# Order of the score products: mask passes first, then row scores, then transposed scores

## The reference

```python
q = query @ wq + query @ Aq @ Bq * 4.0; k = query @ wk; v = query @ wv + query @ Av @ Bv * 4.0
q, k = apply_rope(q), apply_rope(k)                       # per head
scores = einsum('bhqd,bhkd->bhqk', q, k) / sqrt(16)
scores = where(key > query, -1e9, scores)                 # causal
x = layernorm(x + einsum('bhqk,bhkd->bhqd', softmax(scores), v) @ wo)
h = butterfly(gelu(butterfly(x @ W_exp + b_exp, up) + up_bias), down)
x = layernorm(x + h @ W_con + b_con + down_bias)
```

## Time and profile before

| | us |
|---|---|
| median of 3 runs | 1261.94 (1259.41 to 1267.34) |
| the profiled execution, whole | 1255.18 |
| its span on the core | 1253.4 |
| PE busy | 1126.7 (90%) |
| DVE busy | 835.4 (67%) |
| ACT busy | 677.8 (54%) |
| POOL busy | 472.8 (38%) |

### The profile page before, as it was taken

One profiled execution on the slowest core, in us unless ns is written; L12 is line 12 of the kernel. 1 busy time (PEld: TensorE's weight loads), 2 busy tenths in 40 slices (PEclk: granted clock), 3 DMA queues, 4 the chain that ended last, 5 costly groups with the idle time before them and its releaser, 6 DMA issues.

```text
span 1253.4 us, 27298 instructions
## 1 busy us (share of the span) xinstructions
PE 1126.7 (90%) x8462; PEld 787.5 (63%) x8462; DVE 835.4 (67%) x1955; ACT 677.8 (54%) x1067; POOL 472.8 (38%) x536
## 2 busy tenths in 40 slices
PE   4467789999999999999999999999999999989876
PEld 3344456766666666766666666767666666656565
DVE  5497867575767776676767767675767677665332
ACT  1256647465564747465664747365655747474601
POOL 2231334435353444444253434444353434332311
PEclk8678879999999999999999999999999999999989
DMA  5745453645556454644556454645555565641201
GB/s 201 176 143 141 120 146 96 187 122 156 122 148 174 137 154 112 188 124 157 114 165 148 141 151 118 195 112 170 122 165 123 145 164 138 162 117 37 76 21 34
DMA packets 94983, 169.90 MB, mean 136 GB/s; under 512 B 14872, under 2 KB 36120, under 8 KB 94944
## 3 DMA queue, kind: packets, MB, share of 16 engines
q1 hardware_dynamic: 93888, 166.53, 49.3%
q10 hardware_dynamic: 832, 1.83, 0.4%
q0 software_dynamic: 224, 1.04, 0.2%
HBM read 92.28 MB, written 77.07 MB: 135 GB/s over the span
## 4 chain that ended last, share of the span: by engine, by line
PE 73%; DVE 17%; issue 6%; DMA 2%; ACT 2%; POOL 1%; DVEq 0%; POOLq 0%; SPq 0%; ACTq 0%
PE ps_m L516 24%; PE ps_m L659 18%; PE ps_m L629 9%; PE ps_t L601 9%; PE ps_s L558 5%; PE ps_m L638 5%; DVE m_raw L851 4%; PE ps_s L587 2%; DVE m_raw L846 2%; DVE stats L907 2%; DVE x_res L922 1%; DVE rope_in L870 1%; DVE m_pad L860 1%; DVE x1T_lo L878 1%; DVE mv L912 1%
## 5 line engine op out<-in xcount | busy, mean ns | idle before, releaser
L732 ACT ACTIVATE pT<-ps_t 128x512 f32<-128x512 f32 x640 | 345.9, 599 | 275.8 <-PE ps_t L601 275.4
L851 DVE TENSOR_REDUCE m_raw<-ps_s 128x1 f32<-128x512 f32 (+2 forms) x768 | 345.1, 504 | 158.6 <-PE ps_s L587 157.8
L993 POOL TENSOR_SCALAR_AFFINE_SELECT pT<-pT 128x512 f32<-128x512 f32 (+1 forms) x320 | 174.9, 551 | 418.2 <-ACT pT L732 416.0
L659 PE MATMUL ps_m<-w,gact 128*128 128x256 f32 x1024 | 240.4, 386 | 1.8 <-ACT gact L800 1.1
L659 PEld LDWEIGHTS ps_m<-w,gact 128*128 128x128 f32 x1024 | 188.6, 190 | 31.2 <-ACT gact L800 1.5
L558 PE MATMUL ps_s<-k_st,q_st 48*128 48x512 f32 (+3 forms) x1024 | 136.5, 324 | 42.9 <-DVE m_raw L851 24.3
L601 PE MATMUL ps_t<-q_st,k_st 50*128 50x512 f32 (+3 forms) x1024 | 169.0, 388 | 0.5 <-ACT pT L732 0.4
L629 PE MATMUL ps_m<-pT,v_aug 128*32 128x512 f32 (+3 forms) x2048 | 155.6, 445 | 6.5 <-DVE rope_in L870 3.0
L601 PEld LDWEIGHTS ps_t<-q_st,k_st 50*128 50x128 f32 x1024 | 82.1, 186 | 98.7 <-issue 89.4
L558 PEld LDWEIGHTS ps_s<-k_st,q_st 48*128 48x128 f32 x1024 | 95.3, 192 | 53.7 <-DVE m_raw L851 31.9
L629 PEld LDWEIGHTS ps_m<-pT,v_aug 128*32 128x32 f32 x2048 | 58.5, 111 | 83.2 <-issue 79.0
(11 more groups left out here) (112 smaller groups left out, 1582.3 us busy)
## 6 DMA issues: line engine op xcount, KB each, us to landing
qk_scr<-rot_hi SPq DMA_DIRECT2D x64, 512.0 KB, 3.6
q_st<-qk_scr SPq DMA_DIRECT2D x128, 192.0 KB, 4.7
k_st<-qk_scr SPq DMA_DIRECT2D x128, 192.0 KB, 5.2
qk_scr<-rot SPq DMA_DIRECT2D x32, 512.0 KB, 4.1
o_scr<-o_raw SPq DMA_DIRECT2D x64, 256.0 KB, 2.1
r_b<-in_xT SPq DMA_DIRECT2D x17, 512.0 KB, 8.0
o_c<-o_scr SPq DMA_DIRECT2D x32, 256.0 KB
r_b<-r_scr SPq DMA_DIRECT2D x32, 256.0 KB
```

Of the source, the lines that this page charges most:

```text
L659: mm = pe.matmul(pm[:, 0:D], gact[:, k, n * P:(n + 1) * P], w2[:, k, :], start=(k == 0), stop=(k == NHT - 1))
L732: act.activation(pT[:, g % 2, slot, half * T:(half + 1) * T], ps_t[:, ST_BANK[2 * n + r], :], ACT.Exp, scale=SCALE).then_inc(exp_done, 1)
L851: ins = dve.tensor_reduce(m_raw[:, r, u // 2, qt:qt + 1], ps_s[:, r, off:off + (qt + 1) * P], AX.X, ALU.max, negate=True)
L993: pool.affine_select(out=v, in_=v, compare_op=ALU.is_ge, fill=0.0, base=0, pattern=pattern, channel_multiplier=-1).then_inc(mask_done, 1)
```

## The change

In `steps`, "S" comes ahead of "ST" in each step. Within "S" the four mask passes come ahead of the row scores: the first pass of each bank opens it, the second writes the other 64 columns of each diagonal block, and the row-score products add to these and write the rest. `s_done` is signalled by the last row-score product of each bank. The waits stay as they are.

```diff
--- before.py
+++ after.py
@@ -134,8 +134,8 @@
 
         gemms(front, t)
 
+        put("S", *((i, t + LEAD) if t + LEAD < NU else (i + 1, t + LEAD - NU)))
         put("ST", i, t)
-        put("S", *((i, t + LEAD) if t + LEAD < NU else (i + 1, t + LEAD - NU)))
 
         gemms(back, t)
 
@@ -553,26 +553,6 @@
                         pe.wait_ge(fill[g], FILLN * (b + 1))
                     wait(pe, max_done, 2 * (NU * b + n))
 
-                    def s_mm(r, off, x, qt, start):
-                        rows, pr = slice(ROWS * r, ROWS * r + NK), GP * g + x
-                        return pe.matmul(ps_s[:, r, off:off + (qt + 1) * P],
-                                         q_st[rows, pr, qt * P:(qt + 1) * P],
-                                         k_st[rows, pr, 0:(qt + 1) * P], start=start, stop=False,
-                                         skip_group_check=True)
-
-                    if u == GH:
-                        for x in range(GP):
-                            for r in range(2):
-                                s_mm(r, 2 * P * x, x, 1, x == 0)
-                    elif u % 2 == 0:
-                        for r in range(2):
-                            s_mm(r, 0, u // 2, 3, True)
-                    else:
-                        for r in range(2):
-                            s_mm(r, 0, u // 2, 2, True)
-                        for r in range(2):
-                            s_mm(r, 3 * P, u // 2, 0, False)
-
                     for half in range(2):
                         for r in range(2):
                             rows = slice(ROWS * r, ROWS * (r + 1))
@@ -584,10 +564,30 @@
                                 blocks = blocks[:, 1:4:2, :] if u == GH else blocks[:, 2:4, :]
                                 o = blocks[:, :, ROWS * half:ROWS * (half + 1)]
                                 e = eye[rows, :].unsqueeze(1).broadcast_to([ROWS, 2, ROWS])
-                            mm = pe.matmul(o, maskb[rows, half, :], e, start=False, stop=True,
-                                           skip_group_check=True)
-                            if half:
-                                mm.then_inc(s_done, 1)
+                            pe.matmul(o, maskb[rows, half, :], e, start=(half == 0), stop=False,
+                                      skip_group_check=True)
+
+                    def s_mm(r, off, x, qt):
+                        rows, pr = slice(ROWS * r, ROWS * r + NK), GP * g + x
+                        return pe.matmul(ps_s[:, r, off:off + (qt + 1) * P],
+                                         q_st[rows, pr, qt * P:(qt + 1) * P],
+                                         k_st[rows, pr, 0:(qt + 1) * P], start=False, stop=True,
+                                         skip_group_check=True)
+
+                    if u == GH:
+                        for x in range(GP):
+                            for r in range(2):
+                                mm = s_mm(r, 2 * P * x, x, 1)
+                                if x == GP - 1:
+                                    mm.then_inc(s_done, 1)
+                    elif u % 2 == 0:
+                        for r in range(2):
+                            s_mm(r, 0, u // 2, 3).then_inc(s_done, 1)
+                    else:
+                        for r in range(2):
+                            s_mm(r, 0, u // 2, 2)
+                        for r in range(2):
+                            s_mm(r, 3 * P, u // 2, 0).then_inc(s_done, 1)
                 elif kind == "ST":
 
                     g, u = n // UG, n % UG
```

## The result

The changed kernel takes 1270.16 us (median of 11 runs, 1262.55 to 1278.32) against 1260.09 for the kernel before, run beside it: ratio 1.0063, 95% interval 1.0039 to 1.0087 (the two medians alone give 1.0080, inside the interval). So it is slower, by 0.4 to 0.9%. The profiled execution has a span of 1263.2 us instead of 1253.4: +9.8, where the prediction had summed +7.3. The total fits; its parts do not.

A forecast was written before the change was run, and what follows sets the result against it. TensorE was taken as the bound (73% of the chain, 67.4 of about 70 us a batch). Terms 3.4 + 1.4 + 1.5 + 1.0 = +7.3 us on 1255.2 gave 1262.5, scaled to the median 1269; range 1252 to 1284.

The forecast's parts named there:

- Rival 1: Whole kernel faster because waits for the row maxima shrink, at steps 1 and 11: 1246 to 1260 us, chance 0.20.
- rival 2: Masks ahead of the scores expose a TensorE load every step, 0.05 to 0.10 each: 1275 to 1290 us, chance 0.21.
- rival 3: Nothing moves, late and early parts cancel: 1260 to 1263 us, chance 0.12.
- Part 4, the first 190 us: Transposed scores lose their cover in five steps, 0.34 to 0.6 each; earlier maxima give back about 1: +1.0 us.
- Part 1, TensorE: The new product order costs TensorE +0.02 a step over 170 steps: +3.4 us, ends -7 and +8.5.
- Part 3, step 11: Later exponentials delay GpSimd's L993, which holds VectorE's subtraction: +0.10 for 14 batches, +1.4 us.
- the wait before L644 grows by 0.1 to 0.3: TensorE's wait ahead of the transpose of x1, 0.7 in the batch listed, gets longer by this much.
- sign of being wrong: Even step over 0.80 (rival 2), or waits before L621 and L644 under 1.1 and 0.7 a batch (Rival 1).
- other signs: Batches 70.0 to 70.5; even step 0.70 to 0.76; step 0 wait about 0.4; step 1 cast ending with L993 nearly always.
- Part 4, step 0: Transposed scores no longer cover the row scores' wait, +0.23; what is left is 0.21 in 7 batches: +1.5 us.
- the lead of the cast on L993: At step 1, decides whether VectorE's cast gets through before GpSimd's L993: 0.06 lost, 0.10 won.
- GpSimd's run is pinned: At step 1 GpSimd is busy from r_b's arrival (L1008) to L993, whose end small TensorE shifts don't move.

The follow-up runs named there:

- E5: The changed kernel with ScalarE's tmp_x products (L783) moved ahead of the exponentials in batches 0 and 1: 1266.06 us, 1.0035 of the kernel before.
- E1: The kernel before with only the mask passes put ahead of the row scores, transposed scores still first: 1275.39 us, 1.0113 of the kernel before.
- E2: The kernel before with only row scores and transposed scores exchanged, mask passes still last: 1280.71 us, 1.0157 of the kernel before.
- E8: E3 with the whole old order (transposed scores first, mask passes last) at step 0 of every batch: 1261.94 us, 1.0004 of the kernel before.
- E7: E3 with GpSimd's zeroing of the probabilities (L993) listed one step later: 1254.49 us, 0.9937 of the kernel before.
- E10: The kernel before up to batch 1; from batch 2 on the changed order with L993 one step late: 1253.75 us, 0.9942 of the kernel before.
- E11: The kernel before with L993 one step late from batch 2 on and nothing else: 1260.61 us, 1.0001 of the kernel before.
- E3: The changed kernel with transposed scores ahead of row scores again in batches -1 to 1, mask passes first everywhere: 1262.65 us, 1.0025 of the kernel before.
- E6: The kernel before with ScalarE's tmp_x products (L783) moved ahead of the exponentials in batches 0 and 1: 1261.24 us, 1.0004 of the kernel before.

## Why the prediction was right, point by point

The direction, the size and "within 1%" came out. Rival 1 (faster), rival 2 (1275 and up) and rival 3 (1260 to 1263 us) are excluded by the interval. But that the total came out so close (+9.8 for +7.3, 1270 for 1269) is luck: the start was put too low by 6, the batches too high by 5, and 1.7 of the +9.8 is one batch that ran in part at the lower clock.

**Part 4, the first 190 us: the mis-sized term.** Forecast +1.0 with ends -2 and +3, measured +7.1 in the start. I had counted five steps with 0.34 to 0.6 lost each, as if a delay were paid once. It goes round the ring and comes back as the next wait: the waits of the row scores grew by 5.6 us, and more of the start ran at the lower clock. What failed in the prediction is "ScalarE gets its scores 0.3 later and is idle before them, so that costs nothing else": true in a middle batch, false in the start, where VectorE waits for what stands behind the exponentials on ScalarE (E5).

**Part 1, TensorE: right mechanism, wrong end.** I took +0.02 a step, for a step of 0.01 to 0.04 less or up to 0.05 more. Measured is -0.02 in an even step, and 67.01 against 67.43 busy, -0.42 a batch: the lower end. I let the reverse change of type pull me to the middle; its mask load ran only beside its own product, and the float32 load behind bf16 runs ahead of its product. The sum "170 steps times a saving" would have failed too, since nothing of the saving reached the batch.

**Rival 2** was the right mechanism for each half, and the wrong one for both together: the halves change where the masks lie, and only between the two float32 products do they cost a second load.

**Part 3, step 11: right.** The cast gets through and the subtraction is held to 0.02 after L993's end; the wait before L621 is 0.39 against 0.24 before (the one that ends at 601.97), +0.15. I had written 602.02 for 601.91, +0.10. Timeline of after, against the earlier trace rows:

```profile
607.76 0.17 DVE L860 CAST m_pad<-m_raw 128x16 fp32r<-128x16 f32 x1
607.90 0.64 POOL L993 TENSOR_SCALAR_AFFINE_SELECT pT<-pT 128x512 f32<-128x512 f32 x1 [2.33 <-ACT pT L732]
607.97 0.59 DVE L862 TENSOR_TENSOR m_pad<-m_raw,m_pad 128x16 fp32r<-128x16 f32 x1
608.62 0.33 PE L621 MATMUL ps_m<-ident,m_pad 128*128 128x128 f32 x1 [0.39 <-DVE m_pad L862]
```

The forecast that the wait before L644 grows by 0.1 to 0.3 was wrong: 0.4 instead of 0.7, with new waits ahead of the masks in its place. By this the prediction's own sign of being wrong is met (waits before L621 and L644 under 1.1 and 0.7; measured 1.0 and 0.4), though the kernel is not faster. That sign did not count the new waits (0.8). Of the other signs, the even step (0.71) and the wait at step 0 (0.36) came; batches of 70.0 to 70.5 did not (7 of 12 take 69.6 to 69.8), nor the cast held in nearly all of them.

**Part 4, step 0: the wait right, its price wrong.** The wait ahead of the masks is 0.36 (forecast 0.4). Of the +0.21 in seven batches nothing came: in 5 of 12 batches the cast is held to the end of L993 (batches of 70.1 to 70.2), as in 5 of 12 before. Two statements behind it fell. One is "what decides is the lead of the cast on L993: 0.06 lost, 0.10 won". The rows that the lead was read from leave out the GpSimd instruction ahead of L993, the bias addition L1019. Here are two batches of after; in both the cast starts 0.21 ahead of L993:

```profile
641.31 1.29 POOL L1019 TENSOR_TENSOR y<-x_res,bias_out 128x512 f32<-128x512 f32 x1
642.36 0.28 DVE L860 CAST m_pad<-m_raw 128x16 fp32r<-128x16 f32 x1
642.57 0.63 POOL L993 TENSOR_SCALAR_AFFINE_SELECT pT<-pT 128x512 f32<-128x512 f32 x1
642.67 0.55 DVE L862 TENSOR_TENSOR m_pad<-m_raw,m_pad 128x16 fp32r<-128x16 f32 x1
...
851.38 1.34 POOL L1019 TENSOR_TENSOR y<-x_res,bias_out 128x512 f32<-128x512 f32 x1
852.43 0.92 DVE L860 CAST m_pad<-m_raw 128x16 fp32r<-128x16 f32 x1
852.64 0.68 POOL L993 TENSOR_SCALAR_AFFINE_SELECT pT<-pT 128x512 f32<-128x512 f32 x1
```

The cast starts while L1019 still runs. In the first batch it ends 0.04 behind L1019 (642.64 beside 642.60): it was held by L1019 and got through before L993. In the second it is overtaken and ends 0.03 behind L993. In before it is the same (L1019 from 634.54 to 635.86, the cast from 635.74), so a lead on L993 is not what counts. Which of the two waiting instructions gets through when L1019 ends, no run settles. Casts that started 0.04 to 0.07 ahead of L1019's end were always overtaken (E1), those at 0.18 to 0.20 never (E2), those at 0.25 to 0.31 in 5 of 12 batches (after), those at 0.5 never (E8). In before it was 0.08 to 0.12 for the five overtaken ones and 0.14 to 0.15 for the others.

The other is that GpSimd's run is pinned "from the arrival of r_b". It starts when the L993 of step 19 ends; so it did before (627.99 + 0.64 = 628.63, L1008 at 628.59), and with the exponentials coming later, that moved (634.75 + 0.64 = 635.39, L1008 at 635.36):

```profile
634.75 0.64 POOL L993 TENSOR_SCALAR_AFFINE_SELECT pT<-pT 128x512 f32<-128x512 f32 x1 [5.70 <-ACT pT L732]
635.05 1.28 DVE L851 TENSOR_REDUCE m_raw<-ps_s 128x1 f32<-128x512 f32 x2
635.36 1.27 POOL L1008 TENSOR_TENSOR o_c<-o_c,r_b 128x512 f32<-128x512 f32 x1
636.38 0.28 PE L567 MATMUL ps_s<-eye,maskb 64*128 64x128 bf16 x4 [0.36 <-DVE m_raw L851]
```

L1008 starts 0.31 behind the reductions of this place, against 0.13 in the earlier trace rows. The part that held, that L993 and not TensorE ends the waits at the table, is what E7 and E10 confirm, and it is why TensorE's 0.42 brought nothing. The Trainium skill ("SBUF — State Buffer", Who interferes with whom) has whoever issues first hold the port pair for the whole instruction. The cast that ends with L1019 agrees with that, and so does the row at 635.74, which the prediction had read against L993 alone. At the change from L1019 to L993 the order of issue does not decide: the cast was there 0.21 ahead of L993 and in some batches still came second (0.92 at 852.43).

The sum again, measured against forecast: start and front +6.7 for +1.0; batches +1.3 (the one not in the table included) for +6.3; rest +1.8, not forecast, 1.7 of it one batch at a lower clock.

## What to carry to other kernels

Before two independent products change places in an in-order queue, follow what the later one feeds through each engine's queue until you come back to what the earlier one waits for: if the ring closes, a delay can be paid in each round and not once, and the stretch where that engine is short of work shows it, not the middle batch. A saving on the busiest engine is worth nothing while another engine's instruction ends its waits: free that first (here 0.4 a batch came out only then). When types of operands alternate in a block, count the changes that expose a load for the block as a whole; each half of an edit can cost TensorE time (1.1 us a batch here) where the whole edit saves it (0.4).

## What the hardware showed that I had not expected

The same instructions of the start ran at two different granted clocks, in kernels whose code for them is the same. Windows of 40 to 70 us in before and in E11 (length; PE, PEld, DVE, ACT, POOL; granted clock, DMA share, GB/s).

```profile
40.00:70.00 30.00, 20.28 (x113) 15.25 (x113) 14.26 (x29) 5.02 (x18) 0.00 (x0) 0.69 0.79 182
```

```profile
40.00:70.00 30.00, 20.32 (x95) 15.92 (x95) 11.31 (x22) 5.10 (x18) 0.00 (x0) 0.50 0.65 143
```

At 0.50 TensorE stays at 1.2 GHz all the while and does 95 instructions instead of 113; at 0.69 part of the time is at 2.4 GHz. What makes an execution take one or the other, no run says. The first L621 comes at 61.5 to 62.3 us in the executions of before, after, E3, E6 and E10, and at 65.2 to 66.4 in the others, 3 to 5 us later. The rest at the end varies from 158 to 165 us. So single executions of one kernel can differ by more than the whole effect here (the kernel before: 1255 to 1268 us over all its executions), and only cuts at the same instructions or the medians of several runs tell it.
